# Two tiles for the sums of h*C, each sum issued right behind its multiplication, and two tanh buffers instead of three

## The reference

```python
Delta = softplus(combined_delta @ W_tau)
dA = Delta[..., None] * A                      # 16 states per channel
A_bar = exp(dA)
B_bar = expm1(dA) / (dA + 1e-06) * Delta[..., None] * B_proj[:, :, None, :]
def step(h, inp):                              # over the tokens
    a_t, b_t, c_t, u_t = inp
    h = a_t * h + b_t * u_t[..., None]
    y_t = sum(h * c_t[:, None, :], axis=-1)    # the sum over the 16 states
    return h, y_t
out = y * silu(gate) @ W_out + residual
```

## Time and profile before

| | |
|---|---|
| median of 3 runs | 4772.27 us |
| profiled execution | 4775.98 us, span of its instructions 4774.2 us |
| busy share of the span | PE 81%, DVE 85%, ACT 83%, POOL 76% |
| mean granted TensorE clock | 0.885 |

### The profile page before, as it was taken

The page is one execution under the profiler, slowest core; times in us unless marked ns, Lnnn a source line. Parts: engine busy times, 40 slices in busy tenths (PEclk is TensorE's granted clock), DMA queues, the critical chain, the costliest instruction groups (busy, mean ns, idle before and its releaser), DMA issues.

```text
span 4774.2 us, 37136 instructions
## 1 busy us (share of the span) xinstructions
PE 3867.6 (81%) x9708; PEld 1620.4 (34%) x9708; DVE 4043.6 (85%) x3896; ACT 3976.1 (83%) x4394; POOL 3651.3 (76%) x2304
## 2 busy tenths in 40 slices
PE   6624514989898888899898988899898977989889
PEld 3201101334333333333343333333333333333344
DVE  1388799999998989999999989999998998788820
ACT  2688798999989898989989898999899897978811
POOL 0499988888888888788888888788888887767621
PEclk7856756999999999999999999899999998989889
DMA  3678868878787878788787878888887886667541
GB/s 131 218 232 260 247 151 223 223 230 254 223 254 217 257 224 258 213 246 249 224 258 218 250 220 259 238 254 228 238 255 218 240 227 160 181 169 193 154 132 66
DMA packets 352221, 1037.19 MB, mean 217 GB/s; under 512 B 41253, under 2 KB 44389, under 8 KB 344710
## 3 DMA queue, kind: packets, MB, share of 16 engines
q1 hardware_dynamic: 278282, 766.35, 47.0%
q0 software_dynamic: 73728, 268.47, 28.4%
HBM read 639.74 MB, written 126.51 MB: 160 GB/s over the span
## 4 chain that ended last, share of the span: by engine, by line
PE 27%; ACT 21%; issue 14%; DVE 12%; POOL 10%; DMA 8%; SPq 0%; POOLq 0%; DVEq 0%; ACTq 0%
PE ps L1113 11%; PE ps L1132 8%; DMA ysum<-hs 6%; ACT inv L761 4%; PE ps L1083 4%; POOL inv L1379 3%; DVE ps L1179 3%; DVE ps L1167 2%; ACT th L772 2%; DVE ps L1173 2%; ACT inv L754 2%; ACT abar L776 2%; ACT inv L767 2%; POOL hs L1352 2%; DVE hs L1197 1%
## 5 line engine op out<-in xcount | busy, mean ns | idle before, releaser
L1379 POOL TENSOR_TENSOR inv<-inv,th 128x1024 f32<-128x1024 f32 x512 | 1261.4, 2464 | 203.7 <-ACT th L772 202.6
L1113 PE MATMUL ps<-hf,w1r 128*128 128x512 f32 x2304 | 1133.5, 646 | 135.0 <-ACT hT L825 69.9
L1352 POOL TENSOR_TENSOR hs<-hs,Cb 128x1024 f32<-128x1024 f32 x384 | 972.2, 2532 | 34.0 <-DVE hs L1197 17.5
L1150 PE MATMUL ps<-Brow,pick 48*128 48x512 bf16 x1024 | 342.5, 418 | 621.9 <-DVE hs L1197 620.9
L1132 PE MATMUL ps<-w2r,hid 128*128 128x512 f32 x1776 | 815.1, 606 | 0.9 <-DVE x L1236 0.9
L1167 DVE SCALAR_TENSOR_TENSOR ps<-ps,us 128x1024 f32<-128x1024 f32 x512 | 628.4, 1227 | 215.7 <-PE ps L1150 215.4
L754 ACT ACTIVATE inv<-nrd,kappa 128x1024 f32<-128x1024 f32 (+1 forms) x640 | 578.5, 967 | 188.2 <-DVE ps L1179 187.9
L1366 POOL DMA_DIRECT2D ysum<-hs x480 | 437.2, 911 | 355.4 <-DMA ysum<-hs 344.4
L1113 PEld LDWEIGHTS ps<-hf,w1r 128*128 128x128 f32 x2304 | 459.3, 206 | 730.3 <-issue 596.8
L1186 DVE SCALAR_TENSOR_TENSOR ps<-nrd,inv_kappa,ps 128x1024 f32<-128x1024 f32 (+1 forms) x640 | 675.2, 1073 | 15.6
L1197 DVE TENSOR_TENSOR_SCAN hs<-abar,carry,ps 128x512 f32<-128x512 f32 (+1 forms) x384 | 683.6, 1802 | 0.3
(11 more groups left out here) (155 smaller groups left out, 5052.9 us busy)
## 6 DMA issues: line engine op xcount, KB each, us to landing
ysum<-hs POOLq DMA_DIRECT2D x512, 512.0 KB, 5.5
Cb<-c_rows SPq DMA_DIRECT2D x384, 512.0 KB, 4.5
w1r<-in_W SPq DMA_DIRECT2D x144, 512.0 KB, 5.7
w2r<-w_scaled SPq DMA_DIRECT2D x141, 512.0 KB, 7.3
Cb<-c_rows SPq DMA_DIRECT2D x128, 256.0 KB, 3.9
gbc<-expert_gates SPq DMA_DIRECT2D x128, 256.0 KB, 5.2
aw<-in_W_val SPq DMA_DIRECT2D x64, 256.0 KB, 6.5
xa<-in_x SPq DMA_DIRECT2D x32, 512.0 KB, 7.4
```

What stands on the lines that cost most here:

```text
L1113: mm = t.matmul(o, w1r[:, n % 2, k, h * P:(h + 1) * P], hf[:, k, :], start=(k == 0), stop=(k == G - 1))
L1352: gp_.tensor_tensor(hs[:, c % 4, :], hs[:, c % 4, :], Cb[:, c % 2, :], ALU.mult).then_inc(hC_done, 1)
L1379: gp_.tensor_tensor(inv[:, c % 6, :], inv[:, c % 6, :], th[:, c % 3, :], ALU.mult).then_inc(thinv_done, 1)
```

## The change

The sum gets two tiles, one for the even and one for the odd states, with a semaphore each. A sum then waits for the sum of two states before it. `add_to_y` moves from the end of POOL's slot to the place right behind `times_C`, except in the slots with `gate_y`. `gate_y` first adds the odd tile to the even one and waits for that addition, then multiplies by the gate. The second state of a unit is a plain copy too. To make room, `th` has two buffers; the tanh of state c now waits for `weight(c - 2)`.

```diff
-        th = sb("th", [P, 3, TB])
+        th = sb("th", [P, 2, TB])
-        ysum = sb("ysum", [P, TB])
+        ysum = sb("ysum", [P, 2, TB])
...
-                ge(act, thinv_done, c - 2)
+                ge(act, thinv_done, c - 1)
...
-                        dve.wait_ge(y_summed, 16 * (c - 3))
+                        dve.wait_ge(y_summed[c % 2], 16 * (c // 2 - 1))
...
             def add_to_y(c):
                 if 0 <= c < NC:
                     pool.wait_ge(hC_done, c + 1)
-                    if c % N == 0:
+                    if c % N < 2:
                         ge(pool, y_gated, unit(c))
-                        gp_.dma_start(ysum[:], hs[:, c % 4, :]).then_inc(y_summed, 16)
+                        gp_.dma_start(ysum[:, c % 2, :], hs[:, c % 4, :]).then_inc(y_summed[c % 2], 16)
                     else:
-                        pool.wait_ge(y_summed, 16 * c)
-                        gp_.dma_start(ysum[:], hs[:, c % 4, :], accum_op=ALU.add).then_inc(y_summed, 16)
+                        pool.wait_ge(y_summed[c % 2], 16 * (c // 2))
+                        gp_.dma_start(ysum[:, c % 2, :], hs[:, c % 4, :], accum_op=ALU.add).then_inc(y_summed[c % 2], 16)
 
             def gate_y(u):
                 if 0 <= u < NU:
-                    pool.wait_ge(y_summed, 16 * N * (u + 1))
+                    for odd in range(2):
+                        pool.wait_ge(y_summed[odd], 16 * (N // 2) * (u + 1))
+                    gp_.tensor_tensor(ysum[:, 0, :], ysum[:, 0, :], ysum[:, 1, :], ALU.add).then_inc(y_joined, 1)
+                    pool.wait_ge(y_joined, u + 1)
                     pool.wait_ge(gate_ld, 16 * (u + 1))
-                    gp_.tensor_tensor(gy[:], ysum[:], gy[:], ALU.mult).then_inc(y_gated, 1)
+                    gp_.tensor_tensor(gy[:], ysum[:, 0, :], gy[:], ALU.mult).then_inc(y_gated, 1)
...
             times_C(c - 1)
+            if r not in (1, 17):
+                add_to_y(c - 1)
...
             weight(c + 2)
             if r in (1, 17):
                 gate_y(c // N - 1)
-            add_to_y(c - 1)
+                add_to_y(c - 1)
```

More of the change, by code:

```diff
@@ L386, in adaln_mamba_moe @@
             sem("B_ready"), sem("uB_done"), sem("abar_plus_1_done"), sem("weighted_done"), sem("bu_done"), sem("scan_done"))
-        y_summed, y_gated, carry_done = sem("y_summed"), sem("y_gated"), sem("carry_done")
+        y_summed = [sem("even_states_summed"), sem("odd_states_summed")]
+        y_joined, y_gated, carry_done = sem("y_joined"), sem("y_gated"), sem("carry_done")
         a_stat, a_log, a_rstd, a_shift, a_xn = (
@@ L769, in exps @@
                 ins.then_inc(inv_done, 1)
-                ge(act, thinv_done, c - 2)
+                ge(act, thinv_done, c - 1)
                 for cols, g in parts(u):
-                    ins = s.activation(th[:, c % 3, cols], delta[:, u % 2, cols], ACT.Tanh, scale=halfA[:, c % N, g:g + 1])
+                    ins = s.activation(th[:, c % 2, cols], delta[:, u % 2, cols], ACT.Tanh, scale=halfA[:, c % N, g:g + 1])
                 ins.then_inc(th_done, 1)
@@ L1378, in weight @@
                     pool.wait_ge(th_done, c + 1)
-                    gp_.tensor_tensor(inv[:, c % 6, :], inv[:, c % 6, :], th[:, c % 3, :], ALU.mult).then_inc(thinv_done, 1)
+                    gp_.tensor_tensor(inv[:, c % 6, :], inv[:, c % 6, :], th[:, c % 2, :], ALU.mult).then_inc(thinv_done, 1)
             def newton(u, place):
```

## The result

The changed kernel takes 4847.15 us (median of 4 runs, 4840.01 to 4848.89); the kernel before, timed beside it, took 4773.41. The ratio is 1.0154, 95% interval 1.0138 to 1.0171: 74 us slower, where 36 were forecast.

What follows compares the result with a forecast made beforehand. DVE, 94% busy from 800 to 3900 us, was taken to set the pace. Start 13, windows' starts 11 and tanh 12 summed to 36 us slower, giving 4808 us; range 4752 to 4862.

Steps and rivals of the forecast that it cites:

- the tanh's wait: Sign on ACT: the tanh's wait on POOL's weight rises from 0.2 us to 150 or more.
- my case: Main forecast: 36 us slower, 4808 us, spanning 4784 to 4840; chance 0.56.
- the sums' idle time: Sign on POOL: about 0.6 us idle before nearly every sum, near 300 us in all.
- the squares' waits: Sign on ACT: waits at the squares shrink by about as much as the tanh's wait grows.
- DVE's waits for POOL: Sign: they exceed 23 us, above all before 640 us and at the windows' starts.
- The removed wait is worth nothing: POOL's wait on the previous sum's landing, at most 344 us, goes, but nearly all was paid from POOL's lead over DVE.
- 0.62 us of own wait per sum: On POOL, each of 480 moved sums waits for the multiplication in front: 298 us, bounds 0 and 430.
- The addition, 79 us of POOL: One added instruction per unit, 32 of 2.36 us, plus about 0.1 us wait each: 79 us of POOL.
- (b): Each window's start, DVE waiting for POOL's weight: 1 us net per window, 11 us over 11 windows; bounds -5 and 25.
- (a): The start, 280 to 640 us: POOL 20 us later net, of which 13 us counted; bounds 0 and 30.
- (c): ACT's tanh waits for an earlier weight, mostly covered: 1.1 us per window, 12 us over 11 windows; bounds 0 and 33.
- much slower: Rival, 4860 us: ACT and POOL fall into step, 5 us per window lost, start costs 30; chance 0.10.

Runs made afterwards that it cites:

- e13: Changed kernel with the sum back at the slot's end, three tanh buffers, no addition, and halo columns, diagonal tiles and DMA scratch cut: 4772.0 us, ratio 1.0001.
- e10: Changed kernel without the addition of the odd tile to the even one: 4819.0 us, ratio 1.0097.
- e5: Changed kernel with the sum back at the slot's end, three tanh buffers, and halo columns, diagonal tiles and DMA scratch cut: 4791.1 us, ratio 1.0041.
- e4: Changed kernel with three tanh buffers, and halo columns, diagonal tiles and DMA scratch cut to make room: 4816.2 us, ratio 1.0077.
- e14: Changed kernel with three tanh buffers, no addition, and halo columns, diagonal tiles and DMA scratch cut: 4787.0 us, ratio 1.0039.
- e3: Changed kernel with the sum back at the end of POOL's slot, two tanh buffers and the addition kept: 4799.9 us, ratio 1.0047.
- e8: Changed kernel with the sum back at the slot's end, plus a one-column POOL copy behind the multiplication by C that waits for it: 4830.6 us, ratio 1.0119.
- e1: Kernel before with two tanh buffers instead of three, nothing else: 4829.1 us, ratio 1.0109.
- e2: Kernel before with only the sum moved behind the multiplication by C, one sum tile, three tanh buffers: 4994.5 us, ratio 1.0449.
- e17: Kernel before with its three tanh buffers in bfloat16, nothing else: 4758.1 us, ratio 0.9976.
- e12: Changed kernel with the sum back at the slot's end, plus a one-column POOL copy not waiting for the multiplication in front: 4810.7 us, ratio 1.0075.

## Why the prediction was wrong in its size

The direction and a part of what was to be seen came true: no wait on a landing in front of the accumulating sums, the tanh's wait at 197.5 us (150 or more), squares that wait less. The time is inside the stated range and above the 4840 at which "my case" ended. Three signs failed: the sums' idle time is 0.3 us each and 146 us in all, not 0.6 and 300; the squares' waits shrank by a third of the tanh's; and DVE's waits for POOL fell from 23.1 to 13.2 us. The sum of 36 us should have been 74. In the steps' own order:

- *The removed wait is worth nothing.* True in e13 (1.0001), but not for the reason that I had. DVE's stalls behind POOL did go (1.9 us per window) and so did 6.3 us of the start, and the later load in slot 27 ate both. In the changed kernel itself slot 27 isn't longer (7.56 us for 7.78 before): there the load lands in 7.90 us, with two sums in flight for 14% of it.
- *0.62 us of own wait per sum.* Mis-sized. From the multiplication's start to the sum's start it is 2.74 us in the mean of 480 (median 2.67), where a following instruction starts after 2.31: 0.43 us, 208 us in all and not 298. The twin, the plain copy behind the gate, does take 2.95 before and 2.93 after (medians of 31). The 31 cases were one place of the program; I took their cost for all. The Trainium skill (GPSIMD Engine Reference, § 2.1 Instruction dispatch) says that completion holds back only what waits on the instruction's semaphore and not the next POOL instruction; a wait on that semaphore then loses the early start, and the trace agrees, at 0.43 us.

POOL after, around two such sums:

```profile
2104.42 2.62 POOL L1353 TENSOR_TENSOR hs<-hs,Cb 128x1024 f32<-128x1024 f32 x1
2107.34 0.87 POOL L1367 DMA_DIRECT2D ysum<-hs  x1 [0.30 <-POOL hs L1353]
2107.95 2.65 POOL L1447 TENSOR_TENSOR hid<-hid,gbc 128x1024 f32<-128x1024 f32 x1
2110.28 2.65 POOL L1383 TENSOR_TENSOR inv<-inv,th 128x1024 f32<-128x1024 f32 x1
2112.60 2.64 POOL L1353 TENSOR_TENSOR hs<-hs,Cb 128x1024 f32<-128x1024 f32 x1
2115.54 0.88 POOL L1367 DMA_DIRECT2D ysum<-hs  x1 [0.30 <-POOL hs L1353]
```

  This is one of the dearer places, 2.92 us from start to start, of which the view shows only 0.30 as idle.
- *The addition, 79 us of POOL.* Right as work (3732.7 - 3651.3 = 81.4), but I counted its place only at the start. Term (b) lists five sums per window and no addition, though one stands right there, ahead of the gate. It is worth 28 us (e10), 19 with the sum at the end (e13 to e5). This step failed: I asked who waits for the weight, and not who waits for the gate, and so put at nothing the chain of store, load, output projection and DVE's slots 5 to 7, which carries about half of the 28 us in the changed kernel and all that e4's windows are longer than e14's.
- *(a) the start, 13 us.* Measured 7.6 at state 64, within its bounds, and for the reason given: the sum's new place costs 14 to 16 us there (e13 to e14, e3 to the changed kernel) and the removed wait gives 6 to 9.
- *(b) 1 us per window through DVE's waits for the weight.* Wrong in sign: those waits fell from 18.9 to 3.9 us. POOL's lateness reached DVE through the gate (slots 5 to 7) instead.
- *(c) 1.1 us per window through the tanh.* This step failed too: it had 12 us, where the buffer is worth 31 (e4 to the changed kernel). Slots 1 and 23 grew by 3.6 us per window; 0.7 of it stays in slot 23 with three tanh buffers (e4), so 2.9, 32 us, hang on the buffer, where 1.1 were forecast and 3 was the upper bound. The text said that most is covered, because ACT's waits at the squares shrink as the tanh's grow. They shrank by 43 us for 136. The prediction followed one tanh to its DVE wait, at slot 23; the other long one, at the window's start, stands ahead of the convolution's evictions, which I had not looked up. A row of waits of before does name them:

```profile
DVE uu L1250 <- ACT uu L844: 40.6, 8, 17.3
```

  But all eight lie ahead of 183 us, before the windows, and from 800 to 3900 us DVE never waited for them: there the slack had to be read from the order of ACT and the time of DVE's use.

Term by term, added to before in two orders, by the medians:

| step | one order | the other |
|---|---|---|
| wait gone (e13) | -1 | -1 |
| addition | +19 (e5) | +29 (e14 to e4) |
| sum behind C | +47 (e3 to after) | +15 (e14) |
| two tanh buffers | +9 (e5 to e3) | +31 (e4 to after) |
| sum | +74 | +74 |

By the ratios the columns read 0, 19, 51, 3 and 0, 18, 18, 37. So the addition's two sizes can't be told apart. The other two steps are cheap while the rest leaves a lead: the buffer costs 9 us (3) with the sum at the end and 31 (37) behind C, the place 15 us (18) alone and 47 (51) with both others. I sized each against the slack of the kernel before, and added them. The rival "much slower" had 5 us per window, which is what came; but by luck, as neither its condition (0.9 us more per slot of POOL) nor its working (25 us of early tanh per window, all but 5 absorbed) came true: the tanh waited 12 us per window, and the squares absorbed 4.

What stays open: which part of the sum's place beyond e8's 31 us is the issue, which the weight's later end behind it and which the later landing (the median went from 5.5 to 7.8 us, where the sum's issue and SP's load of C both follow the same multiplication); by which path PE's broadcast of B comes late in slot 16 in e1 and in the changed kernel; and what part the lower granted clock has.

## What to carry to other kernels

Slack is one account: size several edits that draw on it together, and follow each delayed instruction to everything queued behind it on every engine that it releases, not only to the waits that the trace already shows. A soft wait of 307 us cost next to nothing at the end of the slot, and moved in front of an operand that others need it grew to 546 us and cost 219 (e2), so where a wait stands matters more than how long it is. When a removed wait brings nothing, look for what it had kept apart: here it spaced two transfers, and with three tanh buffers and no addition a wait in 7 of 32 slots was worth 26 us (with two buffers and the addition 7, within the noise).

## What the hardware showed unexpectedly

- GpSimd's multiplication of two 128x1024 tiles takes 2.36 us in the median with float32 operands and 2.13 with one of them in bfloat16 (e17).
- A GpSimd copy of one column holds the next instruction back by 0.13 us; its wait for the multiplication in front adds 0.19 in the mean (e12, e8).
- With two accumulating transfers of 512 KB in flight for a third of the time, a load of 512 KB took 10.75 us instead of 8.56 (e13, before); with two for 14% of it, it took 7.90 (after), and for 17%, 10.01 (e8).
- The weight's multiplication directly behind the issue of a sum takes 2.65 us in the median (218 in the changed kernel), behind a one-column copy 2.36 (e8).
- A sum's wait for the instruction right in front costs 0.43 us in the mean behind the multiplication by C, and 0.62 in the median behind the gate's.
